# Attention plus ternary FFN on eight cores: the first strip's scores and probabilities in spare buffers, the weight quantisation moved behind the first softmax

## The reference, cut to what matters

```python
def _L0_attn_ref(x, W, b):
    f = jnp.einsum('bsd,hd->bsh', x, W) + b
    e = jnp.einsum('bih,bjh->bij', f, f) + distance_bias(x.shape[1], f.dtype)[None]
    attn = jax.nn.softmax(e, axis=-1)
    return jnp.einsum('bij,bjh->bih', attn, f)

def _L0_ffn_ref(x, weight):                  # weight is made ternary
    scale = jnp.maximum(jnp.mean(jnp.abs(weight)), EPS)
    w_ternary = jnp.clip(jnp.round(weight / scale), -1.0, 1.0)
    return jnp.einsum('bsi,oi->bso', x, w_ternary * scale)

x = x + _L0_attn_ref(_layernorm(x, axis=-1), L0_attn_W, L0_attn_b)
x = x + _L0_ffn_ref(_layernorm(x, axis=-1), L0_ffn_weight)
```

## Time and profile before

| | |
|---|---|
| median of 2 runs | 1307.55 us (1297.57 and 1317.54) |
| profiled execution, device time | 1296.3 us |
| its span, slowest core | 1294.5 us |
| span of the eight cores | 1290.9 to 1294.5 us |
| TensorE matmul busy | 1244.1 us, 96% of the span |
| VectorE busy | 610.4 us, 47% |
| ScalarE busy | 444.5 us, 34% |

### The profile page before, as it was taken

One profiled execution on the slowest core, in us unless ns is written; L12 is line 12 of the kernel. 1 busy time (PEld: TensorE's weight loads), 2 busy tenths in 40 slices (PEclk: granted clock), 3 DMA queues, 4 the chain that ended last, 5 costly groups with the idle time before them and its releaser, 6 DMA issues.

```text
span 1294.5 us, 19544 instructions; the slowest of 8 cores (1290.9 to 1294.5 us)
## 1 busy us (share of the span) xinstructions
PE 1244.1 (96%) x7100; PEld 629.8 (49%) x7100; DVE 610.4 (47%) x944; ACT 444.5 (34%) x664; POOL 12.6 (1%) x29
## 2 busy tenths in 40 slices
PE   3999987999999999999999999999999999999986
PEld 3544445544444444444444444444444444444454
DVE  4666673544444444444444444444444444444442
ACT  5577653233323222233333333322223333333310
POOL 1000000000000000000000000000000000000000
PEclk9899998999999999999999999999999999999999
DMA  9643200001010000000000010001000111111100
GB/s 278 210 128 118 82 1 1 1 33 34 33 33 33 33 23 25 26 27 33 33 33 33 33 33 34 33 33 33 34 33 33 33 33 33 33 33 33 34 33 33
DMA packets 16253, 59.97 MB, mean 46 GB/s; under 512 B 1824, under 2 KB 1824, under 8 KB 16160
## 3 DMA queue, kind: packets, MB, share of 16 engines
q1 hardware_dynamic: 12096, 44.05, 10.3%
q0 software_dynamic: 2912, 10.49, 2.6%
q10 hardware_dynamic: 1152, 4.19, 1.0%
HBM read 41.95 MB, written 16.78 MB: 45 GB/s over the span
## 4 chain that ended last, share of the span: by engine, by line
PE 94%; DVE 2%; DMA 2%; issue 1%; ACT 1%; POOL 0%; DVEq 0%; ACTq 0%; POOLq 0%
PE pb L724 34%; PE pb L918 34%; PE pb L985 9%; PE pb L577 8%; PE pbt L482 7%; DMA wtstage<-wt 2%; PE pb L336 1%; DVE f L114 1%; DVE stats L114 0%; DVE outbuf L114 0%; ACT f L114 0%; DVE lnbuf L114 0%; DVE pT L114 0%; ACT fT L114 0%; POOL wtstage L103 0%
## 5 line engine op out<-in xcount | busy, mean ns | idle before, releaser
L724 PE MATMUL pb<-fT 128*128 128x512 bf16 x2048 | 466.8, 379 | 0.5 <-ACT fT L114 0.5
L918 PE MATMUL pb<-f,pT 128*128 128x512 bf16 x2048 | 447.2, 379 | 0.0
L918 PEld LDWEIGHTS pb<-f,pT 128*128 128x128 bf16 x2048 | 199.1, 98 | 234.1
L724 PEld LDWEIGHTS pb<-fT 128*128 128x128 bf16 x2048 | 195.2, 98 | 213.5 <-issue 0.7
L114 ACT COPY e<-pb 128x512 f32<-128x512 f32 x256 | 150.0, 586 | 205.4 <-PE pb L724 195.5
L114 ACT ACTIVATE p<-e,stats 128x4096 bf16<-128x4096 f32 x32 | 118.7, 3709 | 260.4 <-DVE stats L114 260.4
L114 DVE TENSOR_REDUCE stats<-e 128x1 f32<-128x512 f32 x256 | 175.6, 686 | 29.0 <-ACT e L114 1.6
L114 DVE COPY pT<-pbt 128x1024 bf16<-128x1024 bf16 x128 | 88.5, 692 | 102.9 <-PE pbt L482 98.9
L985 PE MATMUL pb<-wqT,ln2T 128*128 128x512 bf16 x512 | 115.7, 379 | 1.0 <-DVE ln2T L114 1.0
L114 DVE COPY ln2T<-pbt 128x1024 bf16<-128x1024 bf16 x32 | 22.1, 692 | 180.6 <-PE pbt L482 180.6
L482 PEld LDWEIGHTS pbt<-id,p 128*128 128x128 bf16 x1024 | 68.1, 98 | 33.7 <-issue 5.1
(11 more groups left out here) (65 smaller groups left out, 551.7 us busy)
## 6 DMA issues: line engine op xcount, KB each, us to landing
xbuf<-x SPq DMA_DIRECT2D x42, 512.0 KB, 4.3
out<-outbuf SPq DMA_DIRECT2D x32, 512.0 KB, 2.9
out1a<-x SPq DMA_DIRECT2D x8, 512.0 KB, 3.6
xbuf<-x POOLq DMA_DIRECT2D x6, 512.0 KB, 4.1
outbuf<-x POOLq DMA_DIRECT2D x6, 512.0 KB, 4.0
wtstage<-wt ACTq DMA_DIRECT2D x4, 512.0 KB, 14.6
wtstage<-wt POOLq DMA_DIRECT2D x4, 512.0 KB, 19.4
wstage<-ft POOLq DMA_DIRECT2D x4, 512.0 KB, 28.1
```

Of the source, the lines that this page charges most:

```text
L724: return eng.matmul(pb[kb][:, 0:KW], fT[:, hc * S + s * P:hc * S + (s + 1) * P], fT[:, hc * S + h * HALF + kb * KW: hc * S + h * HALF + (k ...
L918: return eng.matmul(fw_ps[nb], pT_sb[:, jt * P:(jt + 1) * P], f_sb[:, jt * D + nb * 512: jt * D + (nb + 1) * 512], start=(jt == 0), stop=( ...
```

## The change

Strip 0 no longer uses `e` and `p`. Its scores go to four spare buffers of 1024 float32 columns (the two `xbuf`, `out1a`, `outbuf`; list `e0alt`) and its probabilities to four of 1024 bfloat16 columns (the two `lnbuf`, `ln2`, `ln2T`; list `palt`). Its exponential is therefore four ScalarE instructions with four partial row sums, which a new VectorE instruction, `v_lsum`, adds up after waiting for the exponential. All eight quantised chunks stand behind `emit_exp(0)`, and so behind `v_lsum`. The waits for the quantisation move from strip 0 to strip 1. The two early x loads wait for strip 0's exponential too, since they write `xbuf`.

```diff
@@ emit_quant_c
             if c == 7:
                 wprep["quant_p"] = done
-            if c == 5:
                 wprep["quant_last"] = done
@@ after the projection
         emit_qpre()
-        for c in (0, 1, 2, 3, 6, 7):
-            emit_quant_c(c)
@@ ahead of emit_e_evacs
+        e0alt = [xb4[0], xb4[1], out1[0], outb]
+        palt = [lnb[0], lnb[1], ln2, ln2T]
+
+        def e_ap(s, bi, r0, r1):
+            if s > 0:
+                lo = (bi // NKB) * HALF + (bi % NKB) * KW
+                return e_sb[:, lo + r0:lo + r1]
+            return e0alt[bi // 2][:, (bi % 2) * KW + r0:(bi % 2) * KW + r1]
@@ emit_e_evacs (the copy, the band and the maximum go through e_ap)
-                    if s == 0 and h == 0 and kb == 0:
+                    if s == 1 and h == 0 and kb == 0:
                         wts.append((s_vq, wprep["quant_e"]))
@@ emit_exp
-            if s == 0:
+            if s == 1:
                 sc_w.append((s_vq, wprep["quant_p"]))
             if s > 0:
                 sc_w.append((s_t, A_done[s - 1]))
+
+            if s == 0:
+                nch = S // D
+
+                def s_exp0(eng):
+                    inst = None
+                    for j in range(nch):
+                        inst = eng.activation(
+                            palt[j][:, 0:D], e0alt[j][:, 0:D], AF.Exp,
+                            bias=st_(NMAX0), scale=1.0,
+                            accum_out=st_(ABS8 + 4 + j))
+                    return inst
+                exp_done[s] = PR.add("scalar", s_exp0, waits=sc_w, inc=s_sx)
+
+                def v_lsum(eng):
+                    return eng.reduce_sum(st_(LSUM0),
+                                          stats[:, ABS8 + 4:ABS8 + 4 + nch],
+                                          AXX)
+                PR.add("vector", v_lsum, waits=[(s_sx, exp_done[s])],
+                       inc=s_vo)
+                return
@@ the passage
         emit_e_mms(0, h_waits=[e0_h0, f_ready_ve])
         emit_e_evacs(0)
         emit_exp(0)
-        for c in (4, 5):
+        for c in range(NH):
             emit_quant_c(c)
@@ emit_A_pack
+                if s == 0:
+                    srcs = [palt[(j0 + j) // (D // P)][
+                        :, ((j0 + j) % (D // P)) * P:
+                        ((j0 + j) % (D // P) + 1) * P] for j in range(n)]
@@ the x loads of the attention
+                if s <= 1:
+                    xw.append((s_sx, exp_done[0]))
                 xl = x_load(NST + s, xw)
```

More of the change, by code:

```diff
@@ L747, in emit_e_evacs, with s_ec @@
                         wts.append((s_sx, exp_done[s - 1]))
-                    if s == 0 and h == 0 and kb == 0:
+                    if s == 1 and h == 0 and kb == 0:
                         wts.append((s_vq, wprep["quant_e"]))
-                    def s_ec(eng, kb=kb, lo=lo, hi=hi):
-                        return eng.copy(e_sb[:, lo:hi], pb[kb][:, 0:KW])
+                    def s_ec(eng, s=s, kb=kb, bi=bi):
+                        return eng.copy(e_ap(s, bi, 0, KW), pb[kb][:, 0:KW])
                     got = PR.add("scalar", s_ec, waits=wts, inc=s_ve)
@@ L760, in v_pm @@
                             eng.tensor_tensor(
-                                e_sb[:, bc0:bc1], e_sb[:, bc0:bc1],
+                                e_ap(s, bi, bc0 - lo, bc1 - lo),
+                                e_ap(s, bi, bc0 - lo, bc1 - lo),
                                 band[:, u0:u0 + (bc1 - bc0)], ALU.add)
-                        return eng.reduce_max(st_(PM0 + bi), e_sb[:, lo:hi],
-                                              AXX)
+                        return eng.reduce_max(st_(PM0 + bi),
+                                              e_ap(s, bi, 0, KW), AXX)
                     PR.add("vector", v_pm,
@@ L825, in emit_A_pack @@
                 n = min(8, NJT - j0)
-                srcs = [p_sb[:, (j0 + j) * P:(j0 + j + 1) * P]
-                        for j in range(n)]
+                if s == 0:
+                    srcs = [palt[(j0 + j) // (D // P)][
+                        :, ((j0 + j) % (D // P)) * P:
+                        ((j0 + j) % (D // P) + 1) * P] for j in range(n)]
+                else:
+                    srcs = [p_sb[:, (j0 + j) * P:(j0 + j + 1) * P]
+                            for j in range(n)]
                 dst = pT_sb[:, j0 * P:(j0 + n) * P]
```

## The result

The changed kernel takes 1315.54 us (median of 7 runs), the kernel before 1296.40 (median of 6, measured beside it). The ratio is 1.0147 with an interval of 1.0134 to 1.0161: 19.1 us, 1.5% slower, and the interval leaves out 1 as well as 1.02. The forecast was 1314.4.

The account below looks back on a forecast made before the run. TensorE, busy 96% of the span, was taken as the bound. Fourth strip 18.5 us later, less 0.4 up to strip 1's scores, gave +18.1 us on 1296.3: 1314.4 us, range 1307 to 1328.

Parts of the forecast that it names:

- The wait in front is worth nothing: Ahead of strip 0's exponential: removing six chunks and a wait gains 0 us, since the exponential depends on the last score matmul.
- The split exponential, +1.43 us: Strip 0's exponential on ScalarE: four pieces in steps of 1.33 us end 1.43 us later; bounds +0.9 and +1.6.
- `v_lsum` ahead of the chunks: On VectorE: it waits for the exponential, so chunk 0 starts at 197.73 us; maxima were done at 191.85.
- Eight chunks ahead of the copy, the main term: On VectorE: eight chunks take 18.0 us, so the second strip's copy starts 19.3 us later and the fourth strip goes 18.5 later.
- The clock: TensorE after the hole: low, rising 5.8 us after strips resume, at 222.4, just before strip 1's scores; bounds -1.3 to +3 us.
- The rest, 0 us: Early x loads, strip 1's waits for chunks and everything after strip 1's scores start: no added time, all shifts alike.
- Rival 1: Quantisation behind the exponential costs nothing where it stands; only the longer exponential's +1.4 us remains, 1297.7 us; chance 5%.
- Rival 2: VectorE without its backlog of six chunks lets strip 0's exponential start earlier; at best -11.5 us, 1285 us; chance 4%.
- Rival 3: 1.2 GHz lasts through strip 1's scores, adding 14 us to their matmuls: +32 us in all, 1328 us; chance 6%.
- The bound of 11.5 us: TensorE's idle time from 191 to 233 us, 7.8 + 3.7, taken as all a perfect passage could give back; 0.9% of span.
- the 226 that the prediction had as a sign of being wrong: Passage in the changed kernel's profile: a low clock lasting beyond 226 us would show the forecast wrong.

Follow-up runs that it names:

- Experiment 7: Kernel before, with all eight quantised chunks in front of strip 0's scores and none behind the exponential: 1299.99 us, ratio 1.0026.
- experiment 3: Changed kernel's spare buffers and four-piece exponential alone, chunks placed as in the kernel before, `v_lsum` behind the last two: 1298.64 us, 1.0013 of the kernel before.
- experiment 1: Changed kernel with `v_lsum` moved behind the eight quantised chunks: 1309.26 us, 1.0096 of the kernel before.
- Experiment 5: Changed kernel with chunks 0 to 3 in front of strip 0's scores and only 4 to 7 behind `v_lsum`: 1307.77 us, 1.0084 of the kernel before.
- Experiment 4: Changed kernel with the copies of the ten transposed strips all on ScalarE: 1299.97 us, 1.0028 of the kernel before.
- experiment 9: Kernel before, strips between score groups, seven f copies and two chunks ahead of strip 1's first maximum, packs later: 1283.30 us; repeated 1284.53, ratio 0.990 both times.
- experiment 2: Changed kernel with the eight chunks moved behind the ten transposed strips and their copies: 1303.08 us, 1.0051 of the kernel before.
- the version with the strips in the gaps: Kernel before, with transposed strips put one or two at a time between the score groups of strips 0 and 1: 1294.95 us, ratio 0.9989.
- experiment 6: Changed kernel with 100 float32 filler matmuls between the third and fourth transposed strip: 1321.38 us, 1.0187 of the kernel before.
- experiment 10: Changed kernel with 60 float32 filler matmuls between the third and fourth transposed strip: 1338.71 us, repeated 1339.71 us.

## Why the prediction was right, point by point

Times from the first score matmul of strip 0, core 1 of the changed kernel (173.61 taken off), and as forecast (176.02 taken off):

| step | forecast | measured |
|---|---|---|
| exponential starts | 16.04 | 16.33 |
| exponential over | 21.27 | 21.57 |
| `v_lsum` starts | 21.44 | 21.74 |
| first chunk | 21.71 | 22.00 |
| VectorE's first f copy | 39.71 | 40.01 |
| fourth strip | 40.55 | 40.85 |
| strip 1's scores | 47.1 | 48.0 |
| product with f (median of cores) | 75.2 | 75.6 |

- **The wait in front is worth nothing**: right. It went, and the exponential started no earlier. Experiment 7 shows how near the limit it was: six chunks fit, eight cost 3.4 us.
- **The split exponential, +1.43 us**: right. Four steps of 1.33 us, 5.24 in all, and +1.7 us with nothing else changed (experiment 3). There was also a pause of 0.3 us ahead of it that nobody forecast (last section). The estimate from the Trainium skill (ScalarE: Activation LUTs, What ACT_TABLE_LOAD costs) would have made it 0.7 us less. The overlap that it counts on is not there in this trace: each piece's sum is read out (0.19 us), and the next piece starts 0.09 us after that.
- **`v_lsum` ahead of the chunks**: right, a wait of 5.56 us, and 5.5 us of hole gone without it (experiment 1).
- **Eight chunks ahead of the copy, the main term**: right. From first chunk to f copy 18.01 us. Experiment 5 halves it and TensorE's hole goes from 17.01 to 7.99 us. Experiment 4 takes the copies out from behind it and keeps all the rest, and 15.5 us go.
- **The clock**: the mechanism was right and the size somewhat off. The granted clock fell to half in the wait and stayed there. I had it rise 5.8 us after the fourth strip; on core 1 it rose at 223.4, 8.9 us after it (0.50 from 222 to 223, 0.80 from 223 to 224), so this core's scores of strip 1 took 14.86 us instead of 13.98 and started 0.9 late. That lies within the bound that I gave it (3 us). Cores 3 and 7 did the same (9.6 and 9.1 us); on core 3, with its times moved onto those of core 0 before, the clock was low until 226.5, just past the 226 that the prediction had as a sign of being wrong. On the other five cores it rose 3.1 to 5.3 us after the fourth strip, and core 0 had its scores at the full clock, 13.98 us.
- **The rest, 0 us**: nearly. The two x loads go at 195.26 and nobody waits for them. The steady strips are unchanged. The rest behind the passage added 1.3 us on the median core and 1.5 on the slowest, which the sum did not have.
- **Rival 1** (the quantisation costs nothing where it stands) fell in the wait of 17.01 us for "DVE f". **Rival 2** (the freed front helps) fell with the exponential at 16.33. **Rival 3** (the clock stays low) fell too: 0.9 us lost in the scores of core 1 and 1.2 in those of core 3, not 14.
- **The bound of 11.5 us** on what a perfect passage could give back was too low: experiment 9's passage is 12.4 us shorter. It counted the idle time alone. TensorE also worked for about 4.9 us at half the clock between 197.1 and 202.9, of which the full clock would give back about 2.4 (an estimate from the windows there). It was the price of rival 2, whose chance does not hang on it.

The forecast for the whole was 18.1 us; the passage grew by 18.2 and the kernel by 19.1. The main terms each came out within 0.3 us, which is not luck. That the whole came within 1.1 us partly is: the sum was taken from core 0, which started strip 0's scores later than any other (176.02 us, the others 171.95 to 174.05), while the core that sets the time of the changed kernel started 2.4 us earlier and lost more by its clock and in its rest.

## What to carry to other kernels

Before work is moved "out of the way" on an engine that is half idle, list what is queued behind its new place and who waits for that: the cost is set by the position in the queue, not by the engine's load. What the same eight chunks cost TensorE in waiting went by what stood behind them: nothing where only copies with time to spare did (experiment 4), 3.84 us with strip 1's score copy behind them (experiment 2), 3.4 us with strip 0's maxima (experiment 7), and 11.5 us, or 17.0 with `v_lsum` ahead, with a copy that frees a PSUM window (experiment 1 and the changed kernel). An instruction that waits for another engine belongs behind the ready work, not ahead of it: `v_lsum` in its first place cost 5.5 us, and in the version with the strips in the gaps that order, together with later packs, made a gain of 12 us out of 1.4.

## What the runs showed that I had not expected

- The last reduction of strip 0's maxima started 0.46 us after the maximum ahead of it in the changed kernel, on all eight cores, and in experiments 1, 2, 4, 6 and 10; it was 0.10 before and in experiments 3 and 5. In experiment 7 a pause of the same 0.46 us stands in the middle of a quantised chunk instead. Nothing in the profile shows a wait there. It made the exponential 0.3 us late; I did not look for its cause.
- The clock comes back at a different time on each core of the same execution. From the strip that ended the longest wait to the rise it took 3.7 to 11.3 us on the eight cores of the kernel before, 3.1 to 9.6 in the changed kernel and 10.5 to 13.2 in experiment 4, where it rose only under strip 1's scores. What came before the rise was the same packs of transpositions in all three. The tables of windows don't say why it differs. By it the same code took 34.2 to 36.5 us from the fourth strip to the product with f on different cores, and the slowest core is one of those where it came late.
- Filler matmuls in float32 are dear: 60 of 128x128x128 took 14.80 us and 100 took 23.48, about 0.24 us each.
